# Fewer copies of the query and key pieces in DRAM, and each half stack loaded in three transfers

## The reference, cut to what matters

```python
q = (x @ Wq + bq).reshape(B, S, N_HEAD, HEAD_DIM).transpose(0, 2, 1, 3)
k = (x @ Wk + bk).reshape(B, S, N_HEAD, HEAD_DIM).transpose(0, 2, 1, 3)
v = (x @ Wv + bv).reshape(B, S, N_HEAD, HEAD_DIM).transpose(0, 2, 1, 3)
scores = jnp.einsum('bhqd,bhkd->bhqk', q / math.sqrt(HEAD_DIM), k)
scores = scores + attention_bias
scores = jnp.where(src_mask, -jnp.inf, scores.astype(jnp.float32))
probs = jax.nn.softmax(scores, axis=-1).astype(v.dtype)
ctx = jnp.einsum('bhqk,bhkd->bhqd', probs, v)
```

## Time and profile before

| | us |
|---|---|
| device time, median of 3 runs (lowest, highest) | 1041.93 (1038.78, 1044.15) |
| span of the profiled execution, first to last instruction | 1036.6 |
| median less span | 5.3 |
| attention | from about 39 to 714 |
| network and the later layers | the rest, not touched |

### The profile page before, as it was taken

How to read it: one execution, slowest core, us unless ns; L and a number is a source line. 1 busy time by engine, 2 the same in 40 slices (tenths; PEclk the granted TensorE clock), 3 DMA queues, 4 the chain that set the end, 5 groups by cost and what they waited for, 6 DMA issues and landing times. The chain is left out here.

```text
span 1036.6 us, 20438 instructions
## 1 busy us (share of the span) xinstructions
PE 956.1 (92%) x5892; PEld 640.9 (62%) x5892; DVE 813.7 (78%) x2075; ACT 734.7 (71%) x1211; POOL 726.3 (70%) x596
## 2 busy tenths in 40 slices
PE   5879999999999999999999999898999999999963
PEld 4646556656655655755665665454777777777752
DVE  8887797878879879879787887874456877887697
ACT  3577887888798788788788878875446556655433
POOL 3487697788788878878778878777555567755631
PEclk9989999999999999999999999999999999999987
DMA  7978978997996997897799799752111111111001
GB/s 262 334 289 292 381 289 278 363 347 238 346 384 214 336 386 257 291 390 292 265 372 343 237 348 370 252 193 82 41 41 41 42 33 50 42 41 41 21 21 41
DMA packets 127535, 230.33 MB, mean 222 GB/s; under 512 B 5488, under 2 KB 53872, under 8 KB 123632
## 3 DMA queue, kind: packets, MB, share of 16 engines
q1 hardware_dynamic: 127472, 229.60, 62.0%
HBM read 187.63 MB, written 41.94 MB: 221 GB/s over the span
## 5 line engine op out<-in xcount | busy, mean ns | idle before, releaser
L937 ACT ACTIVATE prob<-prob,nmax 128x512 f32<-128x512 f32 x512 | 357.0, 729 | 59.6 <-DVE nmax L762 56.4
L762 DVE CUSTOM_DVE_ANT_0 prob<-s_bank,big 128x512 f32<-128x512 f32 x512 | 338.7, 684 | 69.7 <-POOL big L1101 40.3
L1101 POOL TENSOR_TENSOR big<-big,mterm_early 128x2048 f32<-128x2048 f32 (+2 forms) x88 | 305.3, 3484 | 71.5 <-DMA big<-in_fside_Bx16xSxS 62.3
L593 PEld LDWEIGHTS t_bank<-ident,prob 128*128 128x128 f32 x2048 | 238.1, 141 | 168.3 <-issue 51.5
L593 PE MATMUL t_bank<-ident,prob 128*128 128x128 f32 x2048 | 317.7, 278 | 15.9 <-ACT prob L937 6.7
L944 ACT COPY pt<-t_bank 128x512 f32<-128x512 f32 x312 | 181.1, 584 | 51.7 <-PE t_bank L593 50.6
L581 PE MATMUL s_bank<-stack_k,stack_q 128*128 128x512 bf16 x512 | 195.4, 382 | 1.3 <-DVE nmax L762 0.7
L771 DVE COPY pt<-t_bank 128x512 f32<-128x512 f32 x200 | 137.2, 686 | 34.9 <-PE t_bank L593 34.6
L2052 POOL TENSOR_TENSOR gl<-big,gh 128x512 fp32r<-128x512 f32 x64 | 84.6, 1329 | 69.8 <-DVE gh L1643 69.8
L607 PE MATMUL o_bank<-pt,val 128*32 128x512 f32 x1024 | 122.9, 598 | 1.2 <-ACT pt L944 0.7
L1905 ACT ACTIVATE big<-bank,late 128x512 f32<-128x512 f32 x62 | 42.7, 689 | 75.2 <-PE bank L1446 71.4
(11 more groups left out here) (257 smaller groups left out, 1610.0 us busy)
## 6 DMA issues: line engine op xcount, KB each, us to landing
big<-in_fside_Bx16xSxS SPq DMA_DIRECT2D x128, 1024.0 KB, 8.0
pieces_dram<-pieces SPq DMA_DIRECT2D x64, 384.0 KB, 7.3
stack_q<-pieces_dram SPq DMA_DIRECT2D x15, 1024.0 KB, 8.3
stack_k<-pieces_dram SPq DMA_DIRECT2D x15, 1024.0 KB, 10.0
pieces_dram<-pieces SPq DMA_DIRECT2D x32, 256.0 KB, 7.6
xin<-in_x SPq DMA_DIRECT2D x8, 512.0 KB, 8.7
x_dram<-x SPq DMA_DIRECT2D x8, 512.0 KB, 2.6
x1r<-x_dram SPq DMA_DIRECT2D x8, 512.0 KB, 4.3
```

The source lines that it names most:

```text
L593: last = pe.transpose(t_bank[n % 2][:, c * P:(c + 1) * P], prob[:, n % NT, c * P:(c + 1) * P], ident[:])
L762: dve.tensor_tensor_reduce(out=prob[:, n % NT, :], in0=s_bank[n % 3][:, :], in1=bias[:, h % NB, t, :], scale=-1.0, scalar=3e38, op0=ALU.ad ...
L937: act.activation(tile, tile, ACT.Exp, bias=nmax[:, n % NT:n % NT + 1], scale=-1.0).then_inc(exped.sem, 1)
L1101: pool.tensor_tensor(bias[:, h % NB, tiles], bias[:, h % NB, tiles], mterm[:, tiles], ALU.add).then_inc(masked.sem, 1)
```

## The change

The order of the eight products changes, so that the query pieces read 0, 1, 2, 0, 1, 2, 0, 1 and the key pieces 1, 2, 0, 2, 0, 1, 0, 1. Both lists are made of three runs of neighbours in a short list in DRAM: queries 0, 1, 2 and keys 0, 1, 2, 0, 1. DRAM keeps these three and five pieces in place of eight each. A half of the queries is stored with one DMA (384 KB), a half of the keys with two (384 and 256 KB). A half stack is loaded with three DMAs, of rows 0 to 47, 48 to 95 and 96 to 127 (384, 384 and 256 KB).

```diff
-PRODUCTS = [(0, 0), (0, 1), (0, 2), (1, 0), (1, 1), (1, 2), (2, 0), (2, 1)]
-NP8 = len(PRODUCTS)
+PRODUCTS = [(0, 1), (1, 2), (2, 0), (0, 2), (1, 0), (2, 1), (0, 0), (1, 1)]
+KEPT = 5
+RUNS = [(0, 48, (0, 1)), (48, 96, (0, 2)), (96, 128, (0, 0))]
+PIECE_STORES = (16, 32)
...
-                    for i, n in enumerate((3, 3, 2)):
-                        src = pieces[:, qk, i:i + 1].to_broadcast([P, n, S]) if qk == 0 else pieces[:, qk, 0:n]
-                        sp.dma_start(pieces_dram[qk, c, 3 * i:3 * i + n].rearrange("i p t -> p i t"), src
+                    for at, n in ((0, 3), (3, 2))[0:1 + qk]:
+                        sp.dma_start(pieces_dram[qk, c, at:at + n].rearrange("i p t -> p i t"), pieces[:, qk, 0:n]
                                      ).then_inc(pieces_out[c][qk].sem, 16)
+
+            def load_runs(c, qk, heads, arrived):
+
+                for low, high, at in RUNS:
+                    src = pieces_dram[qk, c, at[qk]:at[qk] + (high - low) // HD].rearrange("i (e h) t -> (i e) h t", e=HD)
+                    sp.dma_start((stack_q, stack_k)[qk][low:high, c * HC + heads.start:c * HC + heads.stop], src[:, heads]
+                                 ).then_inc(arrived, 16)
...
-                src = pieces_dram[qk, c].rearrange("i (e h) t -> (i e) h t", e=HD)
-                sp.dma_start((stack_q, stack_k)[qk][:, c * HC:(c + 1) * HC], src).then_inc(stack_in[c].sem, 16)
+                load_runs(c, qk, slice(0, HC), stack_in[c].sem)
...
-                for i, n in enumerate((3, 3, 2)):
+                for i, n in enumerate((1, 1, 1) if qk == 0 else (2, 2, 1)):
                     sp.wait_ge(piece_made, 3 * qk + i + 1)
-                    to = slice(3 * i, 3 * i + n) if qk == 0 else slice(i, NP8, 3)
+                    to = slice(i, i + 1) if qk == 0 else slice(i, KEPT, 3)
```

More of the change, by code:

```diff
@@ L344, in attention_block @@
         cut_done = Count(sem("cut_done"), 4, 4)
-        pieces_out = [[Count(sem(f"pieces_out{c}{qk}"), 48, 48) for qk in range(2)] for c in range(DC)]
-        stack_in = [Count(sem(f"stack_in{c}"), 16 * 2, 16 * 2) for c in range(DC)]
+        pieces_out = [[Count(sem(f"pieces_out{c}{qk}"), PIECE_STORES[qk], PIECE_STORES[qk] if c else 48) for qk in range(2)] for c in range(DC)]
+        stack_in = [Count(sem(f"stack_in{c}"), 16 * 2 * len(RUNS), 16 * 2 * len(RUNS)) for c in range(DC)]
         vst_done = Count(sem("vst_done"), 2, 2)
@@ L464, in load_stack @@
                     apart(sp, sp_apart)
-                sp.wait_ge(pieces_out[c][qk].sem, pieces_out[c][qk].at(b, 48))
+                sp.wait_ge(pieces_out[c][qk].sem, pieces_out[c][qk].at(b, PIECE_STORES[qk]))
                 apart(sp, sp_apart)
-                src = pieces_dram[qk, c].rearrange("i (e h) t -> (i e) h t", e=HD)
-                sp.dma_start((stack_q, stack_k)[qk][:, c * HC:(c + 1) * HC], src).then_inc(stack_in[c].sem, 16)
+                load_runs(c, qk, slice(0, HC), stack_in[c].sem)
             def store_first_pieces(qk):
-                for i, n in enumerate((3, 3, 2)):
+                for i, n in enumerate((1, 1, 1) if qk == 0 else (2, 2, 1)):
                     sp.wait_ge(piece_made, 3 * qk + i + 1)
-                    to = slice(3 * i, 3 * i + n) if qk == 0 else slice(i, NP8, 3)
+                    to = slice(i, i + 1) if qk == 0 else slice(i, KEPT, 3)
                     sp.dma_start(pieces_dram[qk, 0, to].rearrange("i p t -> p i t"),
@@ L478, in load_first_stack @@
             def load_first_stack(qk, heads, arrived):
-                sp.wait_ge(pieces_out[0][qk].sem, pieces_out[0][qk].at(-1, 48))
-                src = pieces_dram[qk, 0].rearrange("i (e h) t -> (i e) h t", e=HD)
-                sp.dma_start((stack_q, stack_k)[qk][:, heads], src[:, heads]).then_inc(arrived, 16)
+                sp.wait_ge(pieces_out[0][qk].sem, pieces_out[0][qk].at(-1, PIECE_STORES[qk]))
+                load_runs(0, qk, heads, arrived)
             def store_x1(b):
@@ L566, in scores @@
                 if first and n == 0:
-                    pe.wait_ge(first_heads_in, 2 * 16)
+                    pe.wait_ge(first_heads_in, 2 * 16 * len(RUNS))
                 elif n % (STEPS // 2) == 0 or first and n == QT * FIRST_HEADS:
@@ L728, in _ @@
             keep_busy(pe, o_bank, wh["wq"][:, 0], 25)
-            pe.wait_ge(pieces_out[0][1].sem, pieces_out[0][1].at(-1, 48))
+            pe.wait_ge(pieces_out[0][1].sem, pieces_out[0][1].at(-1, PIECE_STORES[1]))
             keep_busy(pe, o_bank, wh["wq"][:, 0], 25)
@@ L874, in cut @@
                 if u >= 2:
-                    dve.wait_ge(pieces_out[0][u % 2].sem, pieces_out[0][u % 2].at(-1, 48))
+                    dve.wait_ge(pieces_out[0][u % 2].sem, pieces_out[0][u % 2].at(-1, PIECE_STORES[u % 2]))
                 high, mid, low = (pieces[:, u % 2, i, :] for i in range(3))
@@ L1047, in cut @@
                 before = pieces_out[c - 1][qk]
-                pool.wait_ge(before.sem, before.at(b - 1 if c == 0 else b, 48))
+                pool.wait_ge(before.sem, before.at(b - 1 if c == 0 else b, PIECE_STORES[qk]))
                 high, mid, low = (pieces[:, qk, i, :] for i in range(3))
@@ L2136, in build @@
     x1_dram = nc.dram_tensor("x1_dram", [B, P, DC, S], F32, kind="Internal").ap()
-    pieces_dram = nc.dram_tensor("pieces_dram", [2, DC, NP8, P, S], BF16, kind="Internal").ap()
+    pieces_dram = nc.dram_tensor("pieces_dram", [2, DC, KEPT, P, S], BF16, kind="Internal").ap()
     with ExitStack() as ctx:
```

## The result

The changed kernel takes 1104.67 us (median of 4 runs, 1095.80 to 1109.25), the kernel before 1040.77 beside it (4 runs). The ratio is 1.061 [1.057, 1.064]: slower by 6%, 64 us. I had forecast slower, but 1060 us with a range to 1080. The sign was right and the size was off by more than a factor of three (18 us against 64).

The account below looks back on a forecast made before the run. It took PE, 92% busy, and nearly full DMA in the attention as possible bounds, with late bias loads reaching PE. 1036.6 + 7 x 2.4 + 0.8 = 1054.2, with 5.3 around it about 1060 us; range 1027 to 1080.

Parts of the forecast that it names:

- added DMA time of a load: Loading a half stack as three row ranges was taken to add 2.6 us per load, range 0 to 5.2.
- head 15 late, a batch: The slower first-half loads stand ahead of head 15's bias, so head 15 comes 3.9 us late and PE feels it.
- wait of head 1, credit a batch: At head 1, DVE's 3.70 us wait for POOL was to shrink by 2.05 us; 1.5 us was credited.
- loads of the second half, a batch: Loads at heads 0 and 1, not needed until head 8; their added 5.2 us was counted as nothing.
- around the span: Time outside the profiled span: 5.3 us, added to a span of 1054.2 us to give about 1060.
- The windows move fewer bytes at a full share: Expected profile sign: windows from 435 us would move fewer GB/s while the DMA share stays full.
- The fewer stores: Storing 1.05 MB less saves 2.7 us of DMA time twice a batch; only the store at head 11 was counted.
- the bias loads behind them have slack ... Nothing is counted.: Behind the second half's loads, head 5's bias is the next POOL meets; DVE comes several us later, so zero cost.
- a wait for the bias of head 5 as a sign of being wrong: The prediction listed waits in places counted at nothing, among them the bias of heads 5 and 8, as refuting it.
- idle DMA time near 487: In the window near 487 us DMA share is 0.32; this was to take up the second half's added 5.2 us.
- I credit 1.5 for it.: At head 1, 1.5 us a batch was set against head 15's 3.9 us, leaving 2.4 us net.
- ACT's idle 1.33 us: ACT stands for 1.33 us at head 1's late bias; the 1.5 us credit was this and some DVE lead.

## Why the prediction was right in sign and wrong in size

| term, us | forecast | measured |
|---|---|---|
| added DMA time of a load | 2.6 (0 to 5.2) | 2.6 and 2.9 |
| head 15 late, a batch | 3.9 | 3.9 |
| wait of head 1, credit a batch | 1.5 | 0 (0.6 with the stores alone, most of it at head 4) |
| loads of the second half, a batch | 0 | 3.7 at head 4 |
| clock after the pauses, a batch | not in the sum | 2.0 |
| around the span | 5.3 | 1.8 |

The 5.3 us around the span set a median beside the span of another execution. Where both are of one execution they are 1.8 (1107.34 and 1105.5).

**Right.** The loads are slower because of the partitions that each fills, by the amount taken. The bias of head 15 is late by the forecast time and PE feels it at once. The windows move fewer bytes at a full share. The fewer stores do not make up for it.

**Wrong: "the bias loads behind them have slack ... Nothing is counted."** This step failed and carries most of the miss. Head 5's bias has slack against DVE's use of the mask, as I said, and from the second batch on DVE does not wait for the mask there. I asked only who reads the late result. I did not ask what POOL's late instruction would then lie beside, nor what is queued behind it. It lies beside DVE's normalisation, and the residual copy is queued behind it: 3.7 us a batch where nothing was counted. The prediction had itself named a wait for the bias of head 5 as a sign of being wrong. The second half's loads come in all eight batches too, not in seven. The idle DMA time near 487 that I wanted to let it take up the loads comes too late for it: the stretch of the loads is 0.97 to 1.02 full in the changed kernel, until head 5's bias has landed.

**Wrong: "I credit 1.5 for it."** I had seen that PE has values products there, and put a price on ACT's idle 1.33 us all the same. The run with the stores alone takes away nearly the whole wait, and heads 0 and 1 are no shorter for it. The changed kernel takes 16 us less than the one with eight copies and the same slow loads. That is not 2 us in each of eight batches: the two profiled executions differ by 4.9 us in the first batch, by 3.0 in the last and by 0.9 in the mean of the six between, near the 0.6 of the run with the stores alone. Why the first and the last differ more is open, and the sources in DRAM differ between these two kernels as well.

**Missing: the clock.** A pause of 3 to 4 us at PE costs what it lasts and then some. The windows of a batch give 2.0 us more of PE's busy time for two pauses, and it shows in the heads behind them: head 5 by 0.9, head 15 by 0.7, heads 0 and 1 by 0.4.

The terms as measured, 3.9 + 3.7 + 2.0 = 9.6 for a batch, are near the 9.4 us by which these five batches are longer; with the seventh the mean is 9.2. The first batch is longer by 8.3 and the last by 4.7. With six times 9.2 that makes 68.2, and the span grew by 68.9. The last batch normalises nothing for a next one, and the late loads reach PE in a third way there. A load from `x_dram` is issued behind those of the second half and takes 12.8 us to land where it took 9.7, and PE, which did not wait for it before, waits:

```profile
717.87 1.12 PE L629 MATMUL spare<-ident,proj 128*128 128x128 f32 x4 [2.88 <-DMA proj<-x_dram]
```

What stays open: why the bias of head 5 is later in some batches than in others, so that one way or the other is taken; and why the loads of the second half show somewhat more added time than those of the first.

## What to carry to other kernels

A load that was cut along the free dimension (here by heads) cost nothing more; cut along partitions it cost up to some twice its time, by the ranges that were chosen. A wait is worth what the bounding engine lacks in it: look what that engine does meanwhile before a saved wait is credited. When a DMA makes POOL late, ask not only who reads its result but also what DVE does from SBUF to SBUF at that time and what stands behind it in POOL's queue.

## What the runs showed of the hardware beside this

- One mask of POOL (4.07 us, 128 x 2048, float32) can hold a DVE instruction of 0.41 us for 3.27 us. Under masks a `TENSOR_TENSOR` of DVE with two SBUF operands was slow as well (0.69 to as much as 3.78 us), while its instruction that reads one operand from PSUM and one from SBUF (`prob<-s_bank,big`) never took more than 0.70 us, in 512 of them.
- Beside POOL's short conversions of the mask (0.62 us each, from uint8) one of DVE's normalisations takes 0.775 us, against 0.41 alone.
